# Two orders in a two-layer graph network on one core: the place of the weighted sums in TensorE's slot of stage two, and of ScalarE's reads of the node tile's PSUM in stage one

## What is computed

```python
# layer 0, on h = relu(layernorm(x))
msg = relu(concat(h[src], h[dst], edge_attr) @ W1 + b1) @ W2 + b2
agg = segment_sum(msg, dst)
upd = relu(concat(h, agg) @ U1 + ub1) @ U2 + ub2
x = x + layernorm(h + upd) * gamma + beta
# layer 1, on h = relu(layernorm(x)), with self loops
x_l, x_r = h @ W_l.T + b_l, h @ W_r.T + b_r
z = leaky_relu(x_l[src] + x_r[dst], 0.2)
e = einsum('ehc,hc->eh', z, att)
e = exp(e - segment_max(e, dst)[dst])
alpha = e / segment_sum(e, dst)[dst]
x = x + elu(segment_sum(alpha * x_l[src], dst) + bias)
```

## Time and profile before

| what | us |
|---|---|
| runs | 4942.93, 4945.46, 4946.30 |
| median of the runs | 4945.46 |
| span of the profiled execution | 3996.7 |
| median less span | 948.8 |
| GpSimd busy | 2982.4 (75%) |
| TensorE busy | 3011.3 (75%) |
| gathers of stage one, first to last start | 49.8 to 2010.7 |
| gathers of stage two, first to last start | 2029.0 to 3973.9 |

### The profile page before, as it was taken

How to read it: one execution, slowest core, us unless ns; L and a number is a source line. 1 busy time by engine, 2 the same in 40 slices (tenths; PEclk the granted TensorE clock), 3 DMA queues, 4 the chain that set the end, 5 groups by cost and what they waited for, 6 DMA issues and landing times.

```text
span 3996.7 us, 70006 instructions
## 1 busy us (share of the span) xinstructions
PE 3011.3 (75%) x21068; PEld 2374.6 (59%) x21068; DVE 2040.1 (51%) x8143; ACT 1764.7 (44%) x4359; POOL 2982.4 (75%) x3168
## 2 busy tenths in 40 slices
PE   6777777787777877787767777777777777777776
PEld 5666666666666666666645555555555555555555
DVE  4334343434343434433346666666666666666666
ACT  4333333333333333333345555555555555555555
POOL 6777777777777777777767777777777777777775
PEclk8778787878777878777779999999999999999999
DMA  7445454445444445444433333333333333333332
GB/s 194 135 129 141 132 142 133 137 137 138 136 137 136 137 137 138 136 138 137 117 81 85 87 89 85 90 87 85 88 86 87 86 87 87 87 87 87 86 87 61
DMA packets 339757, 447.03 MB, mean 112 GB/s; under 512 B 152997, under 2 KB 194819, under 8 KB 339375
## 3 DMA queue, kind: packets, MB, share of 16 engines
q1 hardware_dynamic: 239231, 238.02, 20.6%
q0 software_dynamic: 99744, 204.28, 20.2%
q10 hardware_dynamic: 400, 0.20, 0.0%
HBM read 422.13 MB, written 20.07 MB: 111 GB/s over the span
## 4 chain that ended last, share of the span: by engine, by line
POOL 46%; issue 17%; DMA 16%; PE 16%; ACT 5%; DVE 1%; SPq 0%; DVEq 0%; POOLq 0%; ACTq 0%
POOL m_ring L927 31%; POOL t_ring L927 15%; DMA t_ring<-tab_l,src_t 13%; PE bank L2343 3%; PE bank L2322 3%; PE bank L2340 2%; DMA m_ring<-tab_a,src_t 2%; PE bank L2328 2%; PE bank L1583 2%; ACT t_z L2384 1%; ACT t_pen L2386 1%; ACT t_a_edge L2362 1%; PE bank L1575 1%; DVE m_pre L1673 1%; PE bank L1585 0%
## 5 line engine op out<-in xcount | busy, mean ns | idle before, releaser
L927 POOL DMA_INDIRECT m_ring<-tab_a,src_t x1564 | 1485.5, 950 | 488.3 <-issue 475.9
L927 POOL DMA_INDIRECT t_ring<-tab_l,src_t x1553 | 1472.8, 948 | 490.4 <-issue 401.7
L1673 DVE TENSOR_TENSOR m_pre<-bank,m_ring 128x512 f32<-128x512 f32 x391 | 270.4, 692 | 1119.4 <-DMA m_ring<-tab_a,src_t 849.9
L1618 ACT ACTIVATE m_hid<-m_pre 128x512 f32<-128x512 f32 x391 | 246.5, 631 | 1141.9 <-DVE m_pre L1673 1130.7
L2322 PE MATMUL bank<-t_ring,t_a_edge 128*128 128x128 f32 x3106 | 461.0, 292 | 370.0 <-ACT t_a_edge L2362 370.0
L1583 PE MATMUL bank<-w,m_attr_t 128*128 128x128 f32 x3128 | 709.0, 355 | 13.2 <-ACT m_attr_t L1634 13.1
L1583 PEld LDWEIGHTS bank<-w,m_attr_t 128*128 128x128 f32 x3128 | 613.8, 244 | 57.9 <-DVE m_hot L1664 21.0
L2322 PEld LDWEIGHTS bank<-t_ring,t_a_edge 128*128 128x128 f32 x3106 | 385.2, 195 | 423.8 <-ACT t_a_edge L2362 423.8
L2384 ACT ACTIVATE t_z<-bank 128x512 f32<-128x512 f32 x391 | 233.5, 597 | 770.8 <-PE bank L2343 769.1
L2433 DVE TENSOR_TENSOR t_zt<-bank,t_z 128x512 f32<-128x512 f32 x391 | 270.4, 691 | 579.6 <-ACT t_z L2384 579.6
L2328 PE MATMUL bank<-t_zt,att_wn 128*128 128x512 f32 x782 | 413.3, 611 | 2.9 <-DVE t_zt L2433 2.9
(11 more groups left out here) (259 smaller groups left out, 5377.8 us busy)
## 6 DMA issues: line engine op xcount, KB each, us to landing
m_ring<-in_edge_attr_dram SPq DMA_DIRECT2D x390, 256.0 KB
t_rows<-dst_rows SPq DMA_DIRECT2D x196, 256.0 KB
m_rows<-dst_rows SPq DMA_DIRECT2D x196, 192.0 KB
m_ring<-tab_a,src_t POOLq DMA_INDIRECT x1564
t_ring<-tab_l,src_t POOLq DMA_INDIRECT x1553
lone<-tab_l SPq DMA_DIRECT2D x1408, 0.5 KB
m_win<-tab_b SPq DMA_DIRECT2D x391, 24.0 KB
t_win<-tab_r SPq DMA_DIRECT2D x391, 24.0 KB
```

The source lines that it names most:

```text
L927: pool.indirect_dma_start(out=r.got[u][0:rows, j, :], out_offset=None, in_=table, in_offset=bass.IndirectOffsetOnAxis(ap=k.src_t[0:rows, g ...
L1673: dve.tensor_tensor(pre[q % 2][:], p_hid[q % 2][:], r.got[q][:].rearrange("p j d -> p (j d)"), ALU.add).then_inc(s["m_sum"], 1)
```

## The change

Three moves; no instruction is added or removed, and each keeps its wait and its signal. In stage one ScalarE's reads of `p_t` (L1266, L1267) with their wait for `n_d` go from slot 1, where they stood at the head of the slot, to slot 0, behind the copy of the transposed attributes. In stage two TensorE's slot is put into the order turn, logits, own part, output tile, z, weighted sums. VectorE's `own_x` goes behind `zt`, and with it behind the reciprocal of the tail.

```diff
@@ act_tile
             if u == 1 and c is not None:
-                act.wait_ge(s["n_d"], c + 1)
-                act.activation(k.acc[:, 0, cols(c)], p_t[:, 0:P], ACT.Identity, bias=k.bl[:, 0:1])
-                act.activation(tile_zb, p_t[:, P:2 * P], ACT.Identity, bias=k.blr[:, 0:1]).then_inc(s["n_zb"], 1)
                 act.wait_ge(s["n_rows"], c + 1)
...
+        def act_sources(act, rnd, u):
+            c = tile(rnd, 3)
+            if u == 0 and c is not None:
+                act.wait_ge(s["n_d"], c + 1)
+                act.activation(k.acc[:, 0, cols(c)], p_t[:, 0:P], ACT.Identity, bias=k.bl[:, 0:1])
+                act.activation(tile_zb, p_t[:, P:2 * P], ACT.Identity, bias=k.blr[:, 0:1]).then_inc(s["n_zb"], 1)
@@ fast_scalar, stage one
                         act.activation(attr_t[u % 2][:], p_attr[u % 2][:], ACT.Copy).then_inc(s["m_attr"], 1)
+                    act_sources(act, *slot(rnd, u))
                     if tail and u == tail:
@@ and after the rounds
                 act_tile(act, rnd, u)
+                act_sources(act, rnd, u)
@@ fast_tensor, stage two
                         last.then_inc(s["t_turned"], 1)
+                    if at := before(rnd, u, 2, tail):
+                        g, q = at[0] * U + at[1], at[1]
+                        hold(pe, s["t_z"], g + 1)
+                        pe.matmul(p_e[q % 2][:], lhsT=k.att_wn[:], rhs=zt[q % 2][:], start=True, stop=True
+                                  ).then_inc(s["t_ep"], 1)
                     if at := before(rnd, u, 5, tail):
...
-                    if at := before(rnd, u, 4, tail):
...
-                    if at := before(rnd, u, 2, tail):
...
                     if u == 1 and not tail and not (isinstance(rnd, int) and rnd < 3):
                         pe_turn(pe, rnd - 3)
...
                         last.then_inc(s["t_zp"], 1)
+                    if at := before(rnd, u, 4, tail):
+                        g, q = at[0] * U + at[1], at[1]
+                        hold(pe, s["t_at"], g + 1)
+                        for j in range(J):
+                            last = pe.matmul(p_nd[q % 2][:, 3 * W:3 * W + P], lhsT=a_edge[q % 2][:, j, :],
+                                             rhs=column(k, r, g, j), start=(j == 0), stop=(j == J - 1))
+                        last.then_inc(s["t_ndp"], 1)
@@ fast_vector, stage two
-                    if at := before(rnd, u, 5, tail):
...
                     if tail and u == U + 3:
                         dve_rec(dve, rnd - 1)
                     if at := before(rnd, u, 2, tail):
...
                                           ).then_inc(s["t_z"], 1)
+                    if at := before(rnd, u, 5, tail):
+                        g, q = at[0] * U + at[1], at[1]
+                        after(dve, s["t_ndp"], 2 * g + 1)
+                        dve.tensor_tensor(own_x[:], p_nd[q % 2][:, 3 * W:3 * W + P], k.same_head[:], ALU.mult
+                                          ).then_inc(s["t_x"], 1)
```

## The result

The changed kernel takes 4879.14 us (median of 4 runs, 4872.74 to 4882.42), the kernel before beside it 4944.19 (median of 4, 4936.27 to 4946.3): ratio 0.9874, 95% interval 0.986 to 0.9888. It is 65 us faster, where 4945.8 us and no change had been forecast.

The account below looks back on a forecast made before the run. GpSimd (POOL), issuing gathers back to back, was taken to bound both stages. Stage one 0, gathers' pace 0, meetings -1.5 and tail +1.8 made +0.3 us on 4945.46, so 4945.8 us, range 4937 to 4957 us.

Parts of the forecast that it names:

- The step that failed: Whole kernel: the 948.8 us between profiled span and median time were taken as fixed, and terms summed against the span.
- POOL issues back to back through both stages: Both stages: GpSimd's gathers never wait for others, at four gathers and 5.01 us a group.
- Stage one: 0: ScalarE's moved reads: nearly all of TensorE's 166.3 us wait for n_zb goes, but the kernel's end gains 0.
- A stall of 3.6 us never reached them: Stage one: GpSimd's conditions look thirty microseconds and more back, so TensorE's stall of 3.6 us a round cannot delay gathers.
- the loop of 4.46 us: Stage two, old order: z, t_z, t_pen, t_a_edge, weighted sums, logits take 4.46 us a slot, below GpSimd's 5.01.
- The after-loop: Stage two, new order: the loop is TensorE's own work, 3.68 us a slot, allowed 4.0 with hand-overs.
- Meetings of mask and gather, -1.5: Stage two: fewer gathers lengthened by a VectorE mask starting just ahead, -1.5 us, bounds -4.7 and +19.
- tail, +1.8: After stage two's last gather: weighted sums behind z, 0.9 us, and own_x behind the reciprocal, 0.9; +1.8 us, bounds 0 to 2.1.
- The rule of the Trainium skill: VectorE in two-port mode and GpSimd exclude each other for a whole instruction; worst case 137 us, not used in the forecast.
- The marks that were named: Signs of being right: gather spans 1961 and 1945 us, waits for L1267 and t_a_edge gone, L2340's landing wait some 400 us.
- a pace below 1.25 us a gather: Both stages' gathers: a sign that the forecast is wrong and the trace's named waits give a gain.
- Rival (a): Waits named in the trace are real: GpSimd gains 67.3 us in stage two, TensorE's stall goes too; 4878 us, 2%.

Follow-up runs that it names:

- e1: The kernel before, with no edit, run once more against itself: 4939.32 us, ratio 0.9992.
- e9: The changed kernel, with no further edit, against the kernel before at the quick pace: 4002.85 us, ratio 0.9993.
- e2: The kernel before with only stage one's half of the change, ScalarE's two reads moved to slot 0: 4917.79 us, ratio 0.9951.
- e5: The kernel before with three gathers a group instead of four in stage two: 3806.45 us, ratio 0.9523 to the kernel before.
- e10: The changed kernel with three gathers a group instead of four in stage two: 3661.28 us, ratio 0.9142 to the kernel before.
- e11: The changed kernel with three gathers a group in stage two and two of a group's four weighted-sum matmuls left out: 3662.96 us.
- e17: The changed kernel with stage one's four w1 products made twice and stage two's logits three times: 4328.1 us, ratio 1.0822 to the kernel before.
- e6: The kernel before with two unread f32 matmuls added per stage-two slot, ahead of TensorE's wait for t_at: ratio 0.9999 to the kernel before.
- e14: The same edit of the kernel before as e6, run again: ratio 1.0001 to the kernel before.
- e7: The changed kernel with two unread f32 matmuls added per stage-two slot, behind the wait for t_at: ratio 0.9995 to the kernel before.
- e8: The changed kernel with two of a group's four weighted-sum matmuls left out in stage two: ratio 0.9995 to the kernel before.
- e15: The same edit of the changed kernel as e8, run again: ratio 0.9998 to the kernel before.
- e4: The kernel before with TensorE's new order of stage two, but VectorE's own_x left first in its slot: 5169.97 us, ratio 1.0467.
- e13: The same edit of the kernel before as e5, run again: 3807.32 us, ratio 0.9516 to the kernel before.
- e16: The kernel before with stage one's four w1 products made twice and stage two's logits three times: 4476.74 us, ratio 1.1196.
- e18: e16 with three gathers a group instead of four in stage two: 4476.22 us.

## Why the prediction was wrong

**The step that failed** stands at the end of its first part: "The median of the runs is 4945.46 us, 948.8 us more than the profiled span. I take that remainder as fixed, since neither edit is in it, and sum against the span." It isn't a remainder outside the span, but work and waiting inside it. e1 shows a span of 4934.2 us in an execution of 4936.1. The profile at hand was of an execution at the quick pace (3996.7 us, TensorE's granted clock 0.883 on average), the times were of executions at the long pace (clock 0.77). A remainder of 19% of the time, next to no other sign of work around the span, was the warning. A second case, "the profile is of another pace, and the bound may be another engine", belonged among the rivals and wasn't there.

**What followed from it** is that the bound was taken from the wrong pace. "POOL issues back to back through both stages" is right for the profile it was read from, and e9 bears it out: 1940.0 us in stage two, ratio 0.9993. At the long pace it is wrong: in e1 GpSimd waits in 362 places of stage two, and the order on TensorE counts.

**Stage one: 0.** Wrong at the long pace, by 15 us by the traces (24 us by e2's ratio, 15 to 33 by its interval). The chain of the edit was right: n_zb's wait goes (81.1 to 2.7 us by name, 320 to 16 in all), and the reads in slot 0 hold up nobody. "A stall of 3.6 us never reached them" is what failed: GpSimd has then no lead of thirty microseconds to spend, it waits 271.0 us for VectorE's acc in e1, which is downstream of TensorE's slots.

**Stage two: the loop of 4.46 us, 0 while gathers run.** The loop was right to 0.01 us (e5, 4.46), and so was the wait of 370.0 us that it made. The after-loop was put at 3.68, allowed 4.0, measured 4.07 (e10), bounded by the loop through VectorE's and ScalarE's shrink and accumulation to t_zt, and not by TensorE's own work (e10, e11). "Both loops are below POOL's 5.01" holds at the quick pace alone. At the long pace a group takes 2424.1 / 390 = 6.2 us, and the new order gives 0.13 of it, less than the 0.38 of e17. That the old order's loop is the bound there too is seen in a slot of e1, below. Why only a third of its gain comes through is open; the late hand-overs below sit in both orders.

**Meetings of mask and gather, -1.5, and tail, +1.8.** At the quick pace, the only one where they can be told: the mean gather of stage two is 945 ns in e9 against 948 in the earlier trace rows, and the stage 4.9 us shorter, at the lower bound of -4.7 (no meetings). The stretch after the last gather's start is 3992.7 - 3968.4 = 24.3 us, where 24.6 was forecast. In sum -3.4 us for the +0.3 forecast, which the times can't tell from no change. The traces can: stage two takes 1943.3 to 1944.9 us in the three profiles of the old order with four gathers (before, e6, e14) and 1940.0 to 1941.9 in the four of the new (e7, e8, e9, e15), so -3 rather than -1.5, and the stretch at the end 22.8 to 22.9 against 24.3 to 24.8, so the tail's term was right. The rule of the Trainium skill that stood beside this term ("SBUF — State Buffer", section "SBUF: two separate sides") would have allowed 137 us; nothing of that size shows in e9.

**The marks that were named.** L2340's wait for the landing was to rise from 122.0 to some 400 us: 363.7 in e9. L2322's wait for t_a_edge was to go: the weighted sums of e9, L2349 there, have 0.0 us of idle time before them. The mask was to start 4.28 us after z: in a slot of e9 it does so after 4.31 (3024.45 to 3028.76). L1224's wait for L1267 went (5.4 us left in e9). Only "over nearly all slots" fell short, 295 of 391 for the landing. So the marks hold at the quick pace, and the forecast of "no change" is right there. At the long pace they don't: the gathers of the two stages are 2370.4 and 2379.0 us apart for the 1961 and 1945. The sign set against the forecast for a gain, "a pace below 1.25 us a gather", could not show, since the pace was 1.56 us to begin with.

**Rival (a)**, that the waits in the trace are real and come off in the time, gave 4878 us, a microsecond from the result. That is luck: its 67.3 us were GpSimd's gaps of 0.30 us under another name, while the real gain came from two other places, 15 and 49 us.

**Left open.** What makes the long pace, and why the machine shows one or the other for a whole series, these runs don't tell. It isn't the chip alone: e1 to e4 and e13 to e15 are recorded for the same one, less than an hour apart, the first at the long pace, the others at the quick. That the path through TensorE bounds there rests on GpSimd's waits and the slots of e1, on e2 to e4, and on e16 to e18, which rebuild the case at the quick pace; no run took work off GpSimd or TensorE at the long pace itself.

## What to carry to other kernels

Before anything is summed, hold the profiled execution's span against the timed runs: if they differ by more than the microsecond or two that lie around the span here (1.8), the profile shows another regime, and its bound is not the bound of the times. A saving on an engine that only waits less is worth nothing in one regime and something in the other (0.38 us a slot in e17, 0.13 at the long pace), so a forecast of "no change because X bounds" needs the distance to the second bound (here 5.01 against 4.46 us a group, 11%) and a case for what happens if that distance is used up. To find out which loop stands behind a bound, take work off the bounding engine and read the new period: it gave 4.46 and 4.07 us at once.

## What the hardware showed that was not expected

**Two paces of one program.** The kernel before takes 3998 to 4005 us in some series and 4942 in others (at most 0.4% from the median within each), with the granted clock at 0.88 and 0.77 on average. TensorE's granted clock in 40 slices of the span, in tenths of full speed, first in the profile of before, then in e1:

```profile
PEclk8778787878777878777779999999999999999999
```
```profile
PEclk7667666767676676676778888888888888888888
```

The clock of the records alone doesn't make up the difference. TensorE's busy time is 3506.3 us in e1 and 3011.3 in the earlier trace rows, 495 us more, while the span grew by 937.5.

**Late hand-overs from TensorE.** In e1 and in the changed kernel at the long pace, readers of TensorE's results start microseconds after the matmuls' recorded ends. From the timeline of e1:

```profile
3400.93 0.60 PE L2343 MATMUL bank<-ident,t_ring 128*128 128x128 f32 x4
...
3403.26 0.60 ACT L2384 ACTIVATE t_z<-bank 128x512 f32<-128x512 f32 x1 [3.24 <-remote]
3403.50 0.94 POOL L927 DMA_INDIRECT t_ring<-tab_l,src_t  x1 [1.47 <-remote]
```

z ends at 3401.53 by its record, and ScalarE, idle, starts to read it at 3403.26: 1.73 us, where the same pair took 0.04 us in e5. GpSimd's gather, which waits on TensorE too, starts with it. This is what stands behind "remote" in the waits. Whether TensorE stood still, was slower than its records have it, or only its signals were late, they don't say.

The slot that ends with this late hand-over runs from t_z at 3397.10 to t_z at 3403.26, 6.16 us: the 4.43 of the loop, then the 1.73. The next one has no late hand-over. Its chain in e1, and the row of TensorE's granted clock in that stretch (the 0.50, before the DMA share and the GB/s):

```profile
3403.26 0.60 ACT t_z L2384
3403.86 0.61 ACT t_pen L2386
3404.47 0.50 ACT t_a_edge L2362
...
3405.01 2.08 PE bank L2322 x8
3407.08 1.71 PE bank L2328 x2
3408.79 0.43 PE bank L2340
3409.22 0.87 PE bank L2343 x4
```
```profile
3405.01:3410.11 5.10, 5.10 (x17) 3.68 (x18) 2.56 (x13) 1.26 (x5) 2.56 (x3) 0.50 0.23 57
```

It is the loop of the earlier trace rows once more, with the same three steps of ScalarE, and TensorE's four at 1.2 instead of 2.4 GHz: 5.09 us for 2.69, and 6.85 for the slot. So one slot of this pair is long by a late hand-over and the other by the clock, and in both the loop z, t_z, t_pen, t_a_edge, weighted sums, logits is what GpSimd and the slot wait for.

**More TensorE work raised its granted clock.** From 500 to 1500 us in stage one, the changed kernel in e9 and then with the added work in e17 (busy us and instructions of PE, PEld, DVE, ACT, POOL, then the clock):

```profile
500.00:1500.00 1000.00, 788.62 (x6050) 661.37 (x6042) 396.54 (x1344) 331.05 (x923) 756.73 (x799) 0.80 0.49 137
```
```profile
500.00:1500.00 1000.00, 848.40 (x7638) 749.59 (x7631) 397.14 (x1345) 331.20 (x923) 757.03 (x798) 0.94 0.49 137
```

1588 more matmuls in the same stretch cost 59.8 us of busy time, as the mean granted clock went from 0.80 to 0.94 between its levels of 1.2 and 2.4 GHz. At e9's 0.130 us each, 7638 matmuls would have taken 996 of the 1000 us, by my estimate; so the clock gave back most of what the work added, and GpSimd kept the pace of stage one. The Trainium skill says as much in "TensorE: Matmul & The Clock Gate", section "Part 1: The HAM clock gate", that activity releases the throttle, and by that the trace agrees. The reverse shows in e8, where half of the weighted sums was gone and the clock of the whole span was 0.854, against 0.878 in e9.
